# A sixteen-head row of softmax maxima moved in one piece instead of two, with the first sample's PE order rewritten, and the first b and x stores redistributed over the DMA queues

## The reference, cut to what matters

```python
x = x + L0(x)      # q, k, v projections, softmax(q k^T * scale) v, output projection + skip
# L1(x, t_emb):
xr, gate = split(x @ W_in.T); xc = silu(conv4(xr + t_emb)); xn = layernorm(xc) * ln_g + ln_b
Bm, Cm, dt = split(xn @ W_xproj.T)
dt = tanh(dt @ W_dt.T + b_dt) * 0.01
Ad = 1 - dt * tanh(A_log); Bd = Bm * min(|xn|, 1)
h = clip(h * Ad[t] + Bd[t] (x) xn[t], -10, 10); y[t] = Cm[t] . h      # 256 steps, in order
x = x + ((y + D * xn) * silu(gate)) @ W_out.T
```

## Time and profile before

| | |
|---|---|
| median of 3 runs | 540.82 us (540.43 to 543.04) |
| the profiled execution | 541.88 us, span 539.0 us |
| PE busy | 476.7 us (88%) |
| VectorE busy | 431.6 us (80%) |
| ScalarE busy | 256.6 us (48%) |
| GpSimd busy | 171.8 us (32%) |
| mean granted TensorE clock | 0.968 of 2.4 GHz |

### The profile page before, as it was taken

The page is one execution under the profiler, slowest core; times in us unless marked ns, Lnnn a source line. Parts: engine busy times, 40 slices in busy tenths (PEclk is TensorE's granted clock), DMA queues, the critical chain, the costliest instruction groups (busy, mean ns, idle before and its releaser), DMA issues.

```text
span 539.0 us, 8625 instructions
## 1 busy us (share of the span) xinstructions
PE 476.7 (88%) x3064; PEld 288.4 (54%) x3084; DVE 431.6 (80%) x751; ACT 256.6 (48%) x512; POOL 171.8 (32%) x195
## 2 busy tenths in 40 slices
PE   6974998999999989888999887689998999999996
PEld 6842765767676656567898453133333333333333
DVE  6795355777857786849998986899999999999994
ACT  3442476767577646779686765343311111111111
POOL 5145303213031100000640100798783334333332
PEclk8695799999999999999999999999999999999999
DMA  8656374553645620100057547676546433333310
GB/s 311 243 176 169 137 176 100 156 142 97 156 99 148 149 77 1 41 19 21 2 198 242 185 150 168 220 265 199 158 136 135 143 116 117 107 104 104 105 36 22
DMA packets 45606, 71.81 MB, mean 133 GB/s; under 512 B 19097, under 2 KB 34073, under 8 KB 42892
## 3 DMA queue, kind: packets, MB, share of 16 engines
q1 hardware_dynamic: 37556, 64.66, 40.7%
q10 hardware_dynamic: 7480, 3.06, 2.3%
q0 software_dynamic: 528, 3.55, 1.7%
HBM read 41.88 MB, written 23.02 MB: 120 GB/s over the span
## 4 chain that ended last, share of the span: by engine, by line
PE 55%; DVE 27%; DMA 7%; ACT 5%; issue 3%; SPq 1%; POOL 1%; ACTq 1%; another core or an unknown queue 0%; DVEq 0%
DVE win L1926 9%; PE bank L1079 7%; PE bank L1537 6%; PE bank L1137 5%; PE bank L1497 5%; DVE z L1926 5%; PE bank L1508 5%; PE bank L1105 5%; PE bank L1122 4%; PE bank L1196 3%; PE bank L1174 3%; DVE acc L1715 3%; DVE lnb_rep L1926 3%; PE bank L1325 2%; DVE zlast L1926 2%
## 5 line engine op out<-in xcount | busy, mean ns | idle before, releaser
L1737 DVE TENSOR_REDUCE mx<-bank 128x2 f32<-128x512 f32 x128 | 82.0, 685 | 58.1 <-PE bank L1105 57.7
L1497 PE MATMUL bank<-xst,bst 128*128 128x512 bf16 x238 | 76.3, 383 | 22.2 <-DVE win L1926 8.9
L763 ACT ACTIVATE ex<-bank 128x512 f32<-128x512 f32 x128 | 70.8, 599 | 40.7 <-PE bank L1122 40.7
L1926 DVE CUSTOM_DVE_ANT_0 win<-win,bank,hi 128x512 f32<-128x512 f32 x96 | 71.8, 748 | 4.0 <-PE bank L1325 0.7
L1508 PE MATMUL bank<-win,cst 128*32 128x512 f32 x256 | 67.3, 605 | 0.2 <-DVE zlast L1926 0.2
L1497 PEld LDWEIGHTS bank<-xst,bst 128*128 128x128 bf16 x256 | 24.6, 97 | 70.4 <-DVE win L1926 27.4
L1105 PE MATMUL bank<-kst,qst 127*128 127x256 bf16 x256 | 48.6, 283 | 8.1 <-DVE mx L1737 7.2
L1122 PE MATMUL bank<-qst,kst 128*128 128x256 bf16 x256 | 46.5, 275 | 9.8 <-DMA qst<-mT 7.1
L1079 PE MATMUL bank<-xnT,w 128*128 128x256 f32 x192 | 49.2, 410 | 1.7 <-ACT xnT L663 0.9
L517 POOL TENSOR_TENSOR qk<-qk,part 128x512 f32<-128x512 f32 x14 | 16.2, 1156 | 101.3 <-ACT part L678 101.3
L621 POOL TENSOR_TENSOR yg<-yT,gateT 128x128 f32<-128x128 f32 x60 | 29.4, 523 | 56.7 <-ACT yT L1012 56.7
(11 more groups left out here) (218 smaller groups left out, 928.1 us busy)
## 6 DMA issues: line engine op xcount, KB each, us to landing
xs_d<-xpart SPq DMA_DIRECT2D x15, 384.0 KB, 4.8
xst<-xs_d SPq DMA_DIRECT2D x15, 384.0 KB
qk_d<-part SPq DMA_DIRECT2D x58, 96.0 KB, 2.4
xn_d<-xc SPq DMA_DIRECT2D x16, 256.0 KB, 4.0
xtk<-xn_d SPq DMA_DIRECT2D x64, 64.0 KB
xst<-xs_d SPq DMA_DIRECT2D x15, 256.0 KB
bd_d<-zeros POOLq DMA_DIRECT2D x1, 3468.0 KB, 13.1
qst<-qk_d SPq DMA_DIRECT2D x7, 384.0 KB, 3.9
```

Of the source, the lines that this page charges most:

```text
L763: nc.scalar.activation(ex[:, n // 4, n % 4, :], bank[6 + n % 2][:, :], ACT.Exp, scale=SCALE)\
L1497: mm(bank[t % 4][:, :], bst[:, slot, t % RS, :], xst[slot][:, t % RS, :], start=True, stop=True)\
L1737: v.tensor_reduce(mx[:, :, STACKED[n]:STACKED[n] + 1], bank[4 + n % 2][:, :].rearrange("p (t k) -> p t k", t=HALVES), AX.X, ALU.max)\
L1926: v._custom_dve(bass.dve_ops.TENSOR_ADD_SAT, out=zst[t % ZR], in0=zst[(t - 1) % ZR], in1=bank[t % 4][:, :], s0=hi[:, t:t + 1], s1=0.0).the ...
```

## The change

On PE the first half's transposition and its wait go; the order becomes all 16 heads of `max_scores(0)`, `weight_sums`, and `sample(0)`, in which `scores(0, 0, 2)` stands behind the third sample's q and k products, as in the other samples. ScalarE writes one row of 16 maxima, and takes the first two exponentials between the third sample's q and k. SP's loads of `win` and the rest wait for `m_row`. At the hand-over `split` signals after each part; SP stores b 0 to 2 after the first, b 3 after the second, and only then `store_xn(6)`; ScalarE takes over x tile 6 and rows 0 to 7 of tile 7, and stores b 4 and 5 after the third. Gate 5 goes ahead of gate 6, and PE's first scan step waits for both.

```diff
@@ sync @@
-            sp.wait_ge(s["m_half"], 16)
+            sp.wait_ge(s["m_row"], 16)
...
             store_d(0, "bd_first")
-            store_xn(B - 2)
-            store_parts(B - 2)
-            store_parts(B - 1, 0, FIRST, "xs_first")
             sp.wait_ge(s["bsplit"], 1)
             store_b(sp, 0, range(3), 0, RS, "bd_first")
+            sp.wait_ge(s["bsplit"], 2)
+            store_b(sp, 0, (3,), 0, RS, "bd_first")
+            store_xn(B - 2)
             parts_stored(B - 1)
@@ scalar @@
-            def take_first_half():
-                act.wait_ge(s["mt_half"], 1)
-                nc.scalar.activation(mT[0:NH // 2, :], bank[3][0:NH // 2, 0:S], ACT.Copy).then_inc(s["mT_half"], 1)
-                act.wait_ge(s["mT_half"], 1)
-                act.dma_start(qstacks[0][M_ROW:P, 0:NH // 2], mT[0:NH // 2, :]).then_inc(s["m_half"], 16)
...
-                lo = NH // 2 if b == 0 else 0
-                act.dma_start(qstacks[b % NBUF][M_ROW:P, lo:], mT[lo:, :]).then_inc(s["m_row"], 16)
+                act.dma_start(qstacks[b % NBUF][M_ROW:P], mT[:, :]).then_inc(s["m_row"], 16)
@@ sample(b) @@
-                if b == 0:
-                    exponentials(0, 0, 2)
                 if project:
                     take_xn(b + 2, 2)
                 take_maxima(b)
...
                     take_qk(b + 2, 0, 2)
+                    if b == 0:
+                        exponentials(0, 0, 2)
                     take_qk(b + 2, 1, 3)
@@ hand-over @@
-                act.wait_ge(s["gate_done"], {5: 14, 6: 13}.get(b, b * 2 + 2))
+                act.wait_ge(s["gate_done"], b * 2 + 2)
...
             third_part(7)
+            store_parts(act, B - 2)
+            store_parts(act, B - 1, 0, FIRST, "xs_first")
             nc.scalar.activation(warm[:, :], ones[:, 0:1], ACT.Silu)
             act.wait_ge(s["zfill"], 16)
-            act.wait_ge(s["bsplit"], 1)
-            store_b(act, 0, range(3, 6), 0, RS, "bd_first")
+            act.wait_ge(s["bsplit"], 3)
+            store_b(act, 0, (4, 5), 0, RS, "bd_first")
             take_gate(4)
             act.wait_ge(s["bd_first"], 16 * 7)
             load_b(act, 0, "ld_bf", 0, FIRST)
+            take_gate(5)
             take_gate(6)
-            take_gate(5)
@@ tensor @@
             max_scores(0, 0, 8)
-            max_scores(0, 8, 10)
-            turn_first_half()
-            max_scores(0, 10, 14)
-            scores(0, 0, 2)
-            max_scores(0, 14, NH)
+            max_scores(0, 8, NH)
...
                 channels_of(1, 3, "k_done")
-                if b >= 1:
-                    scores(b, 0, 2)
+                scores(b, 0, 2)
                 max_scores(b + 1, 0, 2)
...
+            project_gate(5, 2, 4)
             project_gate(6)
-            project_gate(5, 2, 4)
             project_gate(7, 0, 2)
-            pe.wait_ge(s["bsplit"], 1)
+            pe.wait_ge(s["bsplit"], 3)
...
-            pe.wait_ge(s["gate_out"], 6)
+            pe.wait_ge(s["gate_out"], 7)
             u_steps(0)
@@ vector, split @@
                 for k in range(2):
-                    own.mark(v.tensor_copy(parts[:, k, 0, :], left))
-                    own.settle()
+                    v.tensor_copy(parts[:, k, 0, :], left).then_inc(s[done], 1)
+                    dve.wait_ge(s[done], k + 1)
```

More of the change, by code:

```diff
@@ L257, in build @@
             rt_out xnb_ready tr_done xnT_ready q_done k_done vt_done v_done q_in k_in vt_in v_in cast0 rem_qk
-            cast1 part_ready pw ld_q0 ld_q1 ld_q2 ld_k0 ld_k1 ld_k2 third_ready m_row stacks_clear pw_first ld_half smax_done maxes mt_done mT_ready mt_half mT_half m_half half_gate wx_ready lnb_made
+            cast1 part_ready pw ld_q0 ld_q1 ld_q2 ld_k0 ld_k1 ld_k2 third_ready m_row stacks_clear pw_first ld_half smax_done maxes mt_done mT_ready half_gate wx_ready lnb_made
             st_done exp_done pv_done pvc_ready att_in att_ready skip_done skip_in mix_done x1_ready wcomp wgain pconst xr_done xr_in tap3_ready gate_done
@@ L310, in load_stack, with store_parts @@
                        .then_inc(s[done[w]], 16)
+        def store_parts(eng, j, lo=0, hi=P, done=None):
+            b, t = FINISHED[j]
+            eng.wait_ge(s["parts_ready"], j + 1)
+            eng.dma_start(xs_d[:, b, t * P + lo:t * P + hi, :].rearrange("k p c -> p k c"),
+                          xpart[lo:hi, j % XRING, :, :]).then_inc(s[done or f"xs_out{j % XRING}"], 16)
         block = ctx.enter_context(nc.Block())
@@ L392, in store_xn @@
                 sp.dma_start(xn_d[t * P:(t + 1) * P, b, :], xc[:, b * HALVES + t, :]).then_inc(s[f"xn_out{t}"], 16)
[L394 to L399, removed]
             def parts_stored(tiles):
@@ L436, in _ @@
                 store_xn(j)
-                store_parts(j)
+                store_parts(sp, j)
             sp.wait_ge(s["zfill"], 16)
@@ L448, in _ @@
             load_x(0, "ld_xf", 0, FIRST)
-            store_parts(B - 1, FIRST, RS, "xs_second")
+            store_parts(sp, B - 1, FIRST, RS, "xs_second")
             store_xn(B - 1)
@@ L454, in _ @@
             load_x(0, "ld_x0", FIRST)
-            store_parts(B - 1, RS, P)
+            store_parts(sp, B - 1, RS, P)
             sp.wait_ge(s["ones_in"], 16)
@@ L731, in last_tap @@
                     tap_piece(b, c)
-            def take_first_half():
-                act.wait_ge(s["mt_half"], 1)
-                nc.scalar.activation(mT[0:NH // 2, :], bank[3][0:NH // 2, 0:S], ACT.Copy).then_inc(s["mT_half"], 1)
-                act.wait_ge(s["mT_half"], 1)
-                act.dma_start(qstacks[0][M_ROW:P, 0:NH // 2], mT[0:NH // 2, :]).then_inc(s["m_half"], 16)
             def take_maxima(b):
                 act.wait_ge(s["mt_done"], b + 1)
-                if b == 0:
-                    act.wait_ge(s["m_half"], 16)
                 nc.scalar.activation(mT[:, :], bank[3][0:NH, 0:S], ACT.Copy).then_inc(s["mT_ready"], 1)
                 act.wait_ge(s["mT_ready"], b + 1)
-                lo = NH // 2 if b == 0 else 0
-                act.dma_start(qstacks[b % NBUF][M_ROW:P, lo:], mT[lo:, :]).then_inc(s["m_row"], 16)
+                act.dma_start(qstacks[b % NBUF][M_ROW:P], mT[:, :]).then_inc(s["m_row"], 16)
             def take_weighed(b, par):
@@ L840, in _ @@
             nc.scalar.activation(minus[:, :], ident[:, :], ACT.Copy, scale=-1.0).then_inc(s["minus_ready"], 1)
-            take_first_half()
             for b in range(B):
@@ L1110, in scores @@
             def scores(b, lo, hi):
-                if b == 0 and lo == 0:
-                    pe.wait_ge(s["m_half"], 16)
-                if lo == (NH // 2 if b == 0 else 0):
+                if lo == 0:
                     pe.wait_ge(s["m_row"], b * 16 + 16)
@@ L1145, in turn_maxima @@
                 pe.wait_ge(s["maxes"], b * NH + NH)
-                if b == 0:
-                    pe.wait_ge(s["mT_half"], 1)
                 for t in range(HALVES):
@@ L1150, in turn_maxima @@
                 ins.then_inc(s["mt_done"], 1)
[L1152 to L1158, removed]
             def project_att(b, bk):
```

## The result

| | kernel before | changed kernel |
|---|---|---|
| median | 541.6 us of 9 runs (540.43 to 543.04) | 538.0 us of 9 runs (536.33 to 539.91) |
| profiled execution, its span | 541.88 us, 539.0 us | 538.59 us, 536.8 us |
| head 2's first exponential | 65.59 | 63.20 |
| sample 1's write of maxima issued | 78.73 | 76.35 |
| scan step 0, step 16 on VectorE | 327.55, 341.96 | 326.32, 339.75 |

The changed kernel takes 0.9942 of the time before, 95% interval 0.9921 to 0.9963: 0.58% less, about 3.1 us (the two medians lie 3.6 us apart). The interval lies on both sides of the 0.5% that I had called the border.

The account below looks back on a forecast made before the run. The scan was taken as one VectorE chain that no edit touches, so only the first sample and the scan's start could gain. 3.2 - 0.1 - 0.3 = 2.8 us off the 540.82 median gave 538.0 us, 8-in-10 range 536.4 to 540.4.

Parts of the forecast that it names:

- steps 1 and 2: First sample on PE: without the 6.34 us wait, weight sums start at 46.75 and q products at 51.6, 6.0 us earlier.
- step 3: First sample's row of maxima: write issued at about 51.85, landed at 54.7, covered by the q and k products.
- step 4: Third sample's q and k products: q wholly at the low clock, ready at 55.25; k done at 57.0.
- The early clock: Third sample's q and k products: clock back early, gain 4.0 us instead of 3.2.
- steps 5 and 6: ScalarE: table load (1.29 us) and two exponentials precede k; head 2 starts at 62.4 instead of 65.59, gain 3.2 us.
- step 7: SP's four loads start at 54.8 instead of 50.92; delay to the second sample's stack loads 0 to 1 us, taken as 0.1 loss.
- The hand-over: Start of the scan: tokens stored beside x delay x's first rows; 0.3 us of loss, at most 1.7.
- what moves the series is when x's first rows land: Hand-over: SP's series of loads before scan step 16 shifts only with that landing, 2.75 us after issue before.
- The write stayed fast: Rival on the first sample: maxima write stays slow or clock stays low, giving 538.8 us; chance 0.12.
- the table load didn't drain: Rival on ScalarE's path: the table load drains or an equal wait appears, 1.4 us less gain, 539.4 us; chance 0.06.
- the hand-over took nothing back: Rival at the start of the scan: tokens and x share the engines fully, 1.7 us loss instead of 0.3, 539.4; chance 0.1.
- The clock falls again: Rival before head 2's exponential: PE idles 1.9 us and the clock drops; whole sample low gives 545 to 548 us; chance 0.04.

Follow-up runs that it names:

- e1: The changed kernel with the hand-over as it was before, so only the first sample's edits: 537.88 us, ratio 0.9935.
- e8: The changed kernel with the store of the tokens moved behind the first load of x and the store of rows 8 to 15: one run, 537.65 us.
- e2: The kernel before with only the hand-over's edits, its first sample left as it was: 540.75 us, ratio 0.9993.
- e4: The changed kernel with an early one-element Exp for the table load, and k's copy and cast ahead of the first two exponentials: 538.25 us, ratio 0.9939.
- e5: The changed kernel with matmuls that nobody reads behind each head's maxima of sample 0: 536.19 us, ratio 0.9892.
- e12: Changed kernel with sample 0's unread matmuls, early table load, k first, and half of the third sample's stack stores on ScalarE's queue: 534.15 us, ratio 0.9863.
- e9: The kernel before with unread matmuls behind sample 0's heads 0 to 13 and 84 more in PE's hole: 536.59 us, ratio 0.9908.
- e6: The changed kernel with unread matmuls behind sample 0's heads, early table load, and k ahead of the first two exponentials: 531.81 us, ratio 0.9804.
- e11: Changed kernel with sample 0's unread matmuls, early table load, k first, 92 warm-up matmuls, and an unread matmul behind each of 40 style products: 531.55 us, ratio 0.9815.
- e10: Changed kernel with sample 0's unread matmuls, early table load, k first, and 92 instead of 48 warm-up matmuls: 530.92 us, ratio 0.9807.

## Why the prediction was right, step by step

The reasons hold where the weight lay. That the median is 538.0 us, the forecast to the tenth, is luck: the forecast was 2.8 us off a median of 540.82, while the kernel before gave 541.6 over nine runs, so the medians are 3.6 us apart (3.1 by the ratio, 2.7 in the profiles behind M). In the profiles the first sample gained 0.3 us less than forecast, the stretch behind sample 1's row write lost 0.34 more, and the hand-over came out 0.58 better; these nearly cancel.

- *The hole goes, steps 1 and 2.* Right: shifted by the 0.5 us of M, the weight sums were due at 47.25 and came at 47.45 (by the chain; the timeline, in which matmuls overlap, has 47.24), the q products were due at 52.1 and came at 52.30.
- *The write, step 3.* Issued at 52.53, it landed 3.0 us later, before SP's loads that wait for it start at 55.62; 2.85 us were taken. The q and k products cover it.
- *The clock, step 4.* I had taken q at the low clock and its return behind that. That came true: 3.79 us for the eight products, the clock back between 56 and 57 us. q is copied at 56.12, 0.37 us later than the sum had it; this is the 0.3 us that the gain is short of 3.2. The early clock, up to 0.8 us more gain, did not occur.
- *Table load and k, steps 5 and 6.* The load took 1.28 us and its follower came 1.30 us after its start. By the Trainium skill ("ScalarE: Activation LUTs", What ACT_TABLE_LOAD costs) a drain would have come on top; the trace after shows none either. From the cast of k to head 2 it is 2.43 us again.
- *SP's moved loads, step 7.* The third sample's stack was stored 1.68 us after head 2's exponential in both profiles, so the moved loads cost nothing. But the second sample's row write took 5.18 us instead of 4.72, and that term, taken as 0.1 us, measured 0.44. The bounds of 0 to 1 us held it. It can't be put down to the change: with the same instructions up to there the write took 4.2 us in e1 and 5.3 in e8, and it lands when the stack's loads do, which are issued until 1.31 us ahead of it before, and 1.18, 1.49 and 1.22 us ahead after, in e1 and in e8.
- *The hand-over.* The first link was right (3.04 us against 2.75, 0.3 as predicted), the term was not: the links behind it gave back half by the issue of the last load (333.75 - 213.09 = 120.66 us against 335.53 - 215.02 = 120.51), step 16 found the last loads landed, and the profile has a gain of 0.28 where 0.3 of loss stood. e2 at 0.9993 says that neither can be told from nothing. The step that failed is "what moves the series is when x's first rows land": how long the later links take scatters by more than the 0.3 us (126.51 to 127.36 us with the new hand-over). The sign that I had named for it, step 16 waiting 1 to 2 us, did not appear either: step 0 came 0.70 us later, the cover of 1.27 us was used up, and step 16 waited for nothing.
- *The rivals.* The write stayed fast, the table load didn't drain, the hand-over took nothing back, and the second sample's stack was in time. "The clock falls again" did not happen in the changed kernel's profile at either wait, but did in e4, e5 and e12, behind waits of 1.94 to 2.56 us. As I had it, at a chance of 0.04 and against a single row, it was too lightly dismissed: the change has two such waits, and in the closest variant, e4, one of them cost 1.5 us. On the other side, e1 and e8 have the same two waits as the changed kernel and kept the clock at both, so of this order of work three profiles are known and none with the fall.

What I did not see is what else was to be won. I read the low clock of the first sample as a given that sets durations. It is a loss of its own, and not a smaller one: keeping the clock up is worth 0.9% in the kernel before (e9), where the removed hole is worth 0.6%, with intervals that overlap, and change, fillers and k ahead together give 2.0% (e6).

## What to carry to other kernels

When a stall goes, follow the work that lay inside it for nothing: here a table load and two exponentials moved onto the path and took 2.8 of 6.0 us. Where TensorE runs at its lower clock in a stage that another engine paces, price that first, and try a few idle-time matmuls there before the schedule is rewritten; afterwards look at every wait of about 2 us, since a saving can be lost behind it. For a small write that the next step waits for, look at how long before it the last large load was issued. Don't hand DMA issues to an engine on the path: four of them took 2.57 us here and held up its exponentials for 2.28.

## What the runs showed of the hardware

- *The clock falls while TensorE is stopped in short pieces.* In the maxima stage after, PE is busy 2.04 of 3.80 us and then at 0.50 of its clock; with fillers it is busy 3.61 of 3.80 in the same stage of e6 and keeps 1.00. The windows of e6, to set beside the first two of the changed kernel:

```profile
34.20:38.00 3.80, 3.61 (x39) 2.54 (x37) 3.80 (x7) 0.31 (x1) 1.04 (x1) 1.00 0.77 228
38.20:44.20 6.00, 4.67 (x55) 3.50 (x52) 5.83 (x15) 1.54 (x2) 3.33 (x1) 1.00 0.67 186
```

The Trainium skill ("TensorE: Matmul & The Clock Gate", A second HAM failure mode) describes a kernel whose clock swings because TensorE idles briefly and often between groups of matmuls; this stage agrees as to the short stops; but here the clock did not swing, it fell once near 40 us and stayed low until between 56 and 57 us.

- *The same wait does not always cost the clock.* It fell after 2.21 us in e4, 2.56 in e5 and 1.94 in e12, and held through 2.12 and 2.21 us in the changed kernel, 2.34 in e1, 2.08 in e6, 2.15 and 2.35 in e8 and 2.59 in e11. What decides it stays open.
- *One spell of low clock near the start moves everything behind it.* In 22.00 to 25.40 us the granted clock is 1.00 in the profiles of e2, e6, e8, e9 and e10, and M is 33.14 to 34.24; it is 0.51 to 0.60 in the other eight, before and after among them, and M is 35.14 to 36.00. The instructions ahead of it are the same in most of these kernels. e2's profile is 1.4 us shorter than that of before, and 1.56 us of difference is in M alone: two spans are compared rightly only from a milestone behind it. What brings the spell on was not found. The windows of before and of e6:

```profile
22.00:25.40 3.40, 3.40 (x12) 2.95 (x12) 3.13 (x11) 0.73 (x2) 2.01 (x2) 0.51 0.32 68
```
```profile
22.00:25.40 3.40, 3.40 (x22) 2.86 (x21) 3.06 (x12) 1.08 (x3) 2.01 (x2) 1.00 0.40 94
```

- *A small write behind large loads.* The same 8 KB to one partition took 5.18 us behind loads issued until 1.18 us before it, 1.8 us where they were issued until 5.96 us before it (e12), and 3.0 us in the first sample at a DMA share of 0.05 (1.8 to 3.2 us there over the profiles with one row). Issued less than 2.3 us behind the last of the loads, it landed 5.7 to 6.5 us behind that issue, in all profiles.
